# Cross-attention and mixture of experts: attended columns centred while they are copied, means added back later

## What is computed

```
energy    = (ctx Wq^T + bq) (ctx Wk^T + bk)^T                      # per batch, 256 x 256
x         = x + layernorm(x) @ softmax(energy)^T
logits    = layernorm(x) @ gate^T;  e = argmax;  slot = rank of the token in e (dropped from 160 on)
out[tok]  = x[tok] + prob * gelu(layernorm(x)[tok] @ wi[e]) @ wo[e]
```

## Time and profile before

| | before |
|---|---|
| runs | 110.72, 111.43, 111.35 us |
| the profiled execution, its own time | 110.13 us |
| its span on the core | 108.3 us |
| TensorE busy, share of the span | 101.4 us, 94% |
| VectorE, ScalarE, GpSimd busy | 33.2, 33.0, 31.0 us |
| granted TensorE clock, mean | 0.988 |

### The profile page before, as it was taken

How to read it: one execution, slowest core, us unless ns; L and a number is a source line. 1 busy time by engine, 2 the same in 40 slices (tenths; PEclk the granted TensorE clock), 3 DMA queues, 4 the chain that set the end, 5 groups by cost and what they waited for, 6 DMA issues and landing times.

```text
span 108.3 us, 1960 instructions
## 1 busy us (share of the span) xinstructions
PE 101.4 (94%) x744; PEld 89.9 (83%) x744; DVE 33.2 (31%) x135; ACT 33.0 (30%) x87; POOL 31.0 (29%) x58
## 2 busy tenths in 40 slices
PE   5999999989999989999999999999999999999910
PEld 5875987869999779998998998669989999988900
DVE  0055898999710143600510400220020010011210
ACT  4139678865651302341041041002302303200000
POOL 5710599677770000030200200303003003012550
PEclk9999999999999999999999999999999999999995
DMA  2989999999992879999999999960001001001100
GB/s 74 273 298 355 355 321 408 424 412 420 415 387 100 176 235 377 332 316 396 436 421 415 421 430 414 424 244 33 0 0 42 0 6 48 0 0 47 54 3 3
DMA packets 7713, 25.76 MB, mean 238 GB/s; under 512 B 912, under 2 KB 4245, under 8 KB 5656
## 3 DMA queue, kind: packets, MB, share of 16 engines
q1 hardware_dynamic: 6680, 23.39, 58.2%
q0 software_dynamic: 880, 2.12, 5.3%
q10 hardware_dynamic: 144, 0.13, 0.5%
HBM read 21.14 MB, written 4.76 MB: 239 GB/s over the span
## 4 chain that ended last, share of the span: by engine, by line
PE 75%; DMA 12%; POOL 3%; issue 2%; DVE 2%; SPq 2%; ACT 0%; ACTq 0%
PE ps L822 68%; DMA shared<-in_head 5%; PE ps L866 4%; DMA slots_dram<-rows,slot 4%; DMA rest<-slots_dram 3%; POOL slots_dram L339 2%; PE ps L819 2%; POOL out L377 1%; DVE rows L561 1%; SPq L218 1%; SPq L214 1%; DVE stats L619 0%; DVE stok L746 0%; ACT attended L388 0%; DVE y_end L798 0%
## 5 line engine op out<-in xcount | busy, mean ns | idle before, releaser
L822 PE MATMUL ps<-wo_sb,shared 128*32 128x128 f32 (+2 forms) x320 | 36.4, 337 | 0.0
L822 PE MATMUL ps<-shared,wi_sb 128*128 128x160 f32 x244 | 34.6, 299 | 0.0
L822 PEld LDWEIGHTS ps<-shared,wi_sb 128*128 128x128 f32 x244 | 33.6, 190 | 0.1
L822 PEld LDWEIGHTS ps<-wo_sb,shared 128*32 128x32 f32 (+1 forms) x320 | 29.2, 142 | 5.0 <-issue 0.7
L493 ACT ACTIVATE shared<-ps 128x480 f32<-128x480 f32 (+1 forms) x24 | 12.5, 526 | 48.9 <-PE ps L822 48.4
L370 POOL DMA_INDIRECT out<-y,got x9 | 8.8, 974 | 60.8 <-DVE y L780 44.1
L780 DVE SCALAR_TENSOR_TENSOR y<-ps,share,got 128x256 f32<-128x256 f32 x9 | 4.4, 484 | 48.1 <-PE ps L822 24.7
L822 PE MATMUL ps<-shared 128*128 128x256 f32 (+1 forms) x28 | 9.5, 481 | 0.1
L339 POOL DMA_INDIRECT slots_dram<-rows,slot x8 | 8.2, 1021 | 3.4 <-DVE slot L604 1.9
L822 PE MATMUL ps<-attended,shared 128*128 128x272 f32 x32 | 8.3, 398 | 0.5 <-ACT attended L388 0.5
L822 PEld LDWEIGHTS ps<-shared 128*128 128x128 f32 x28 | 6.0, 229 | 2.2 <-issue 1.0
(11 more groups left out here) (87 smaller groups left out, 72.3 us busy)
## 6 DMA issues: line engine op xcount, KB each, us to landing
wi_sb<-in_wi SPq DMA_DIRECT2D x8, 1024.0 KB, 15.6
wo_sb<-in_wo SPq DMA_DIRECT2D x8, 1024.0 KB, 18.9
slots_dram<-fill SPq DMA_DIRECT2D x1, 1300.0 KB, 12.6
shared<-in_xT SPq DMA_DIRECT2D x2, 512.0 KB, 7.3
out<-rows SPq DMA_DIRECT2D x4, 256.0 KB, 5.6
got<-slots_dram SPq DMA_DIRECT2D x1, 780.0 KB, 6.3
got<-slots_dram SPq DMA_DIRECT2D x4, 130.0 KB, 2.5
shared<-in_x SPq DMA_DIRECT2D x2, 256.0 KB, 4.0
```

The costliest lines, as they stand in the source:

```text
L822: return nc.tensor.matmul(dst, lhsT, rhs, start=(k == 0), stop=last)
```

## The change

The rows that leave `x1` have no mean any more. `idg` and `attended` get one more column beside the eight gate columns (`G` = 9), so that `at` also yields minus the mean of each attended row over its columns. VectorE copies that one column out of PSUM (`column_mean_of(b, c)`), and ScalarE adds it as a bias while it copies (`at`, now an Identity with a bias). GpSimd prepares mean minus input from `mv` alone, and `x1` subtracts it. `bn2`, `st2` and `token` are gone: ScalarE's `squared(n)` makes the sum of squares in one pass, `disp` takes the rows themselves, and the first expert's tokens are copied with no change of sign. The row's mean comes out of the extra column (`mean(b)`) and travels with the row. It is added back in two places: by VectorE to the rows read back from the slots (`full_row`), and by GpSimd to the eight row tiles, after the scatters have landed, before SyncE writes them to the output. `BY_LOG` is 1: batches 1 to 3 get their deviation through logarithm and exponential, only batch 0 through GpSimd. All four `turner` are built by VectorE. The lists of ScalarE, GpSimd, VectorE and TensorE are in another order.

```diff
...
-WIDE = H + 2 * E
-HALF = WIDE // 2
+
+G = E + 1
+HALF = P + G
+WIDE = 2 * HALF
...
-BY_LOG = 3
+BY_LOG = 1
...
             sp.dma_start(got[:, 0, :], by_rank[0:P, 0, :]).then_inc(got_zero, 16)
             sp.dma_start(got[:, 2:E, :], by_rank[0:P, 2:E, :]).then_inc(got_main, 16)
             sp.dma_start(rest[:, 1, :], by_rank[P:CAP, PER_STACK:E, :]).then_inc(rest_here[1], 16)
-            for b in range(B):
-                sp.dma_start(out_v[b], rows[:, 2 * b:2 * b + 2, 0:H]).then_inc(x1_out, 16)
             last_slots(0)
             last_slots(1)
+            for b in range(B):
+                sp.wait_ge(full_rows, 2 * b + 2)
+                sp.dma_start(out_v[b], rows[:, 2 * b:2 * b + 2, 0:H]).then_inc(x1_out, 16)
             for e in range(3, E):
...
+            nc.gpsimd.memset(fill[:, 0:H], 0.0).then_inc(fill_done, 1)
+            nc.gpsimd.memset(fill[:, H:ROW], 1.0).then_inc(fill_done, 1)
+            pool.wait_ge(fill_done, 2)
...
-            nc.gpsimd.memset(idg[:, HALF + E:], 0.0).then_inc(zeroed, 1)
+            nc.gpsimd.memset(idg[:, P + E:P + G], -1.0 / H).then_inc(ident_done, 1)
+            nc.gpsimd.memset(idg[:, P + G + E:HALF + G], -1.0 / H).then_inc(ident_done, 1)
+            nc.gpsimd.memset(attended[:, :, :, E:G], -2.0 / H).then_inc(means_put, 1)
+
+            nc.gpsimd.memset(rows[:, :, MEAN], H ** 0.5 * EPS ** 0.5).then_inc(eps_put, 1)
...
             def shifted_input(n):
-                pool.wait_ge(shift1_done, n // 4 + 1)
-                nc.gpsimd.tensor_scalar(x_sb[:, n, :], x_sb[:, n, :], 1.0, shift1[:, n:n + 1], ALU.mult,
+
+                pool.wait_ge(st1_done, n // 4 + 1)
+                nc.gpsimd.tensor_scalar(x_sb[:, n, :], x_sb[:, n, :], -1.0, mv[:, n, 0:1], ALU.mult,
                                         ALU.add).then_inc(xs_done, 1)
...
             def second_rstd(b):
-                pool.wait_ge(st2_done, b + 1)
-                if b == 0:
-                    pool.wait_ge(filled, 16)
+                pool.wait_ge(square_sums, 2 * b + 2)
                 pair = slice(2 * b, 2 * b + 2)
                 nc.gpsimd.tensor_tensor(rows[:, pair, RSTD], rows[:, pair, RSTD], minus_half[:, 0:2],
                                         ALU.pow).then_inc(rstd2_done, 1)
...
             def scatter(n):
 
+                if n == 0:
+                    pool.wait_ge(filled, 16)
                 if n % 2 == 0:
                     pool.wait_ge(numbered, n // 2 + 1)
+                    pool.wait_ge(mean_put, n // 2 + 1)
                     pool.wait_ge(row_ready[n // 2], 2)
...
-            put_gate()
-            first_rstd(0)
             shifted_input(0)
             shifted_input(1)
+            first_rstd(0)
+            put_gate()
             shifted_input(2)
-            first_rstd(1)
             shifted_input(3)
             shifted_input(4)
             shifted_input(5)
+            shifted_input(6)
             second_rstd(0)
-            shifted_input(6)
             shifted_input(7)
+            first_rstd(1)
             scatter(0)
-            second_rstd(1)
...
+
+
+            pool.wait_ge(scattered, 16 * NT)
+            pool.wait_ge(disp_done, 2)
+            for n in range(NT):
+                nc.gpsimd.tensor_scalar(rows[:, n, 0:H], rows[:, n, 0:H], 1.0, rows[:, n, MEAN:MEAN + 1], ALU.mult,
+                                        ALU.add).then_inc(full_rows, 1)
...
                     act.wait_ge(xm_done, 2 * (b - 1))
                 act.wait_ge(at_done, HC * b + c + 1)
-                copy(attended[:, b % 2, c, E:WIDE], p_at[c][:, E:WIDE]).then_inc(at_sb, 1)
-
-            def turn_by(b):
-
-                act.wait_ge(erec_done, b + 1)
-                act.wait_ge(at_done, HC * (b - 1))
-                for m in range(2):
-                    n = 2 * b + m
-                    nc.scalar.activation(turner[:, b % 2, m * HALF:(m + 1) * HALF], idg[:, m * HALF:(m + 1) * HALF],
-                                         ACT.Copy, scale=erec[:, n:n + 1]).then_inc(act_turner_done, 1)
+
+                act.wait_ge(column_means, HC * b + c + 1)
+                nc.scalar.activation(attended[:, b % 2, c, G:WIDE], p_at[c][:, G:WIDE], ACT.Identity,
+                                     bias=column_mean[:, b, c:c + 1]).then_inc(at_sb, 1)
...
                 pair = slice(2 * b, 2 * b + 2)
-                act.wait_ge(st2_done, b + 1)
+                act.wait_ge(square_sums, 2 * b + 2)
                 nc.scalar.activation(near[:, pair], rows[:, pair, RSTD], ACT.Ln).then_inc(log_done, 1)
                 act.wait_ge(log_done, b + 1 - BY_LOG)
...
-            def token(n):
-
-                act.wait_ge(st2_done, n // 2 + 1)
+            def squared(n):
+
+                act.wait_ge(x1_done, n + 1)
                 if n == 0:
-                    act.wait_ge(en_done, B)
-                nc.scalar.activation(tok[:, n, :], rows[:, n, 0:H], ACT.Identity, bias=rows[:, n, MEAN:MEAN + 1],
-                                     scale=-1.0).then_inc(tok_done, 1)
+                    act.wait_ge(eps_put, 1)
+                if n >= 2:
+                    act.wait_ge(square_sums, n - 1)
+                nc.scalar.activation(squares[:, n % 2, :], rows[:, n, 0:H + 1], ACT.Square, scale=H ** -0.5,
+                                     accum_out=rows[:, n, RSTD:RSTD + 1]).then_inc(square_sums, 1)
...
-            nc.scalar.activation(dispT[:, 1, 0, :], p_disp[1], ACT.Copy, scale=-1.0).then_inc(disp_sb[1], 1)
+            copy(dispT[:, 1, 0, :], p_disp[1]).then_inc(disp_sb[1], 1)
...
                 dve.wait_ge(erec_done, b + 1)
                 if b == 0:
                     dve.wait_ge(gate_done, 1)
-                    dve.wait_ge(ident_done, 2)
+                    dve.wait_ge(ident_done, 4)
+                if b >= 2:
+                    dve.wait_ge(at_done, HC * (b - 1))
                 nc.vector.tensor_tensor(per_half(turner[:, b % 2, :]), per_half(idg[:]),
                                         erec[:, pair_of(b)][:, :, None].to_broadcast([P, 2, HALF]),
                                         ALU.mult).then_inc(turner_done, 1)
 
+            def column_mean_of(b, c):
+
+                dve.wait_ge(at_done, HC * b + c + 1)
+                nc.vector.tensor_copy(column_mean[:, b, c:c + 1], p_at[c][:, HALF + E:HALF + G]).then_inc(column_means, 1)
+
             def x1(n):
+
+                dve.wait_ge(rstd1_done, n // 4 + 1)
                 dve.wait_ge(xm_done, n + 1)
                 dve.wait_ge(xs_done, n + 1)
-                nc.vector.scalar_tensor_tensor(halves(rows[:, n, 0:H]), halves(p_xm[n // 2 % 2][:, n % 2, 0:WIDE])[:, :, E:HALF],
+                nc.vector.scalar_tensor_tensor(halves(rows[:, n, 0:H]), halves(p_xm[n // 2 % 2][:, n % 2, 0:WIDE])[:, :, G:HALF],
                                                rstd1[:, n:n + 1], halves(x_sb[:, n, :]), ALU.mult,
-                                               ALU.add).then_inc(x1_done, 1)
+                                               ALU.subtract).then_inc(x1_done, 1)
...
-                nc.vector.tensor_tensor(logits[:, b, :, :], p_xm[b % 2][:, :, HALF:HALF + E], wide(rstd1[:, pair_of(b)]),
-                                        ALU.mult).then_inc(scaled_done, 1)
+                nc.vector.tensor_tensor(logits[:, b, :, :], p_xm[b % 2][:, :, HALF:HALF + G],
+                                        rstd1[:, pair_of(b)][:, :, None].to_broadcast([P, 2, G]), ALU.mult).then_inc(scaled_done, 1)
...
-            def bn2(n):
-                dve.wait_ge(x1_done, n + 1)
-                nc.vector.bn_stats(stats[:, 1, n, 0:6], rows[:, n, 0:H]).then_inc(bn2_done, 1)
-
-            def st2(b):
-                dve.wait_ge(bn2_done, 2 * b + 2)
-                for n in range(2 * b, 2 * b + 2):
-                    last = nc.vector.bn_aggr(rows[:, n, MEAN:RSTD + 1], stats[:, 1, n, :])
-                last.then_inc(st2_done, 1)
+            def mean(b):
+
+                dve.wait_ge(square_sums, 2 * b + 2)
+                dve.wait_ge(logits_done, b + 1)
+                dve.wait_ge(shift1_done, b // 2 + 1)
+                nc.vector.scalar_tensor_tensor(rows[:, pair_of(b), MEAN], logits[:, b, :, E], -0.5, shift1[:, pair_of(b)],
+                                               ALU.mult, ALU.add).then_inc(mean_put, 1)
...
+            gate()
+            mx(0)
...
+            column_mean_of(0, 0)
...
-                nc.vector.tensor_scalar(stok[:, i % 2, :], row[:, 0:H], row[:, MEAN:MEAN + 1], row[:, RSTD:RSTD + 1],
-                                        ALU.subtract, ALU.mult).then_inc(stok_done, 1)
+                nc.vector.tensor_scalar(stok[:, i % 2, :], row[:, 0:H], row[:, RSTD:RSTD + 1], None,
+                                        ALU.mult).then_inc(stok_done, 1)
...
+            def full_row(n):
+
+                t = OUT_TILES[n]
+                if n == 0:
+                    dve.wait_ge(got_zero, 16)
+                elif n == 1:
+                    dve.wait_ge(got_one, 16)
```

(27 more changed lines are left out.)

168 lines of the change are left out of this document (89 added, 79 removed).

## The result

The changed kernel takes 113.29 us (median of four executions, 112.69 to 114.8) against 111.23 us (median of four, 110.72 to 111.43): a ratio of 1.017, 95% interval 1.0125 to 1.0215. It is slower, by 2.1 us. I had forecast 110.35 us in a range of 109.4 to 111.6.

A forecast was written before the change was run, and what follows sets the result against it. The last scatter's landing was taken as the bound, its chain 0.9 us later than TensorE's. Landing 1.0 us earlier, all else 0, gave 111.35 - 1.0 = 110.35 us, range 109.4 to 111.6.

The forecast's parts named there:

- The walk up to the routing's end: Routing on TensorE and VectorE: `x1(7)` at 24.95, `row_numbers(3)` at 28.0, last `disp` ended at 28.95, 1.2 us earlier.
- The one after `row_numbers` starts 0.43 us after its start ... scatter 4 at 26.0: GpSimd's scatters: scatter 4 at 26.0, then 1.25 or 1.3 us apart, the last at 29.8, 1.25 us earlier than 31.08.
- The sentence on `first_rstd(1)` ending as `row_numbers(0)` starts: GpSimd ahead of the first scatter: `first_rstd(1)` stands there now and ends at 20.1, when `row_numbers(0)` starts.
- I take ... a landing at 34.1: Last scatter's landing: 0.25 us of the 1.25 us gain lost beside streaming weights, so 1.0 us earlier.
- My first rival: At the scatters' landing: the weights hold it, gain 0 to 0.5 us, time 110.85 to 111.35; chance 0.2.
- from 33 to 35 q0 alone was left: DMA queues before the landing: only the scatters' queue still moved then, 0.09 MB at 13.1%.
- The rule that I cited against the change: DMA engines go round their queues packet by packet; in the extreme the landing gains 0 instead of 1.0 us.
- Nothing else is on the path: Beyond landing and TensorE: adding means, output and expert 3's weights are hidden, so 110.13 - 1.0 = 109.1 us.
- The third rival: VectorE's routing: small operations cost 0.2 us, not 0.1, `row_numbers(3)` at 29.8, time 111.75 to 112.5; chance 0.13.

The follow-up runs named there:

- `a_again2`: The changed kernel with nothing altered, measured again on a later occasion: 110.19 us against 110.1 us of before, ratio 1.000.
- `b_again`: The kernel before with nothing altered, run again for its trace on a later occasion: 111.74 us in one execution.

## Why the prediction was wrong

Undisturbed, the forecast of 1.0 us gained turned into 0 at two steps, the issue of the scatters and their landing.

**The walk up to the routing's end** was close: measured from the start of `at(0)` (10.88 before, 10.14 after, 10.76 in `a_again2`), `x1(7)` comes at 14.6 where I had 14.07, `row_numbers(2)` at 15.2 where I had 14.67, `chosen(3)` at 16.5 where I had 16.0. Half a microsecond of 16 too early, in both traces alike. TensorE started `mm1(0)` 0.64 us earlier and not 1.2.

**"The one after `row_numbers` starts 0.43 us after its start ... scatter 4 at 26.0"** failed. I used that distance for scatter 4 and never walked scatters 0 to 3. They stand on the same engine at 1.28 us each, the third waited for ScalarE's `expz(1)`, which ended 1.1 us later than before, and from there GpSimd had no pause left: 27.08, and 30.92 for the last, 0.16 us gained and not 1.25. ScalarE's list was never walked for what a scatter needs. The sentence on `first_rstd(1)` ending as `row_numbers(0)` starts asked only whether GpSimd is free, not what else the scatters wait for.

**"I take ... a landing at 34.1"** failed: 35.8 and 35.1. My first rival was right, the weights hold the landing, and I gave it 0.2. The premise "from 33 to 35 q0 alone was left" was a misreading. The view of the earlier trace rows for 33 to 35 us has one line more:

```profile
q1 hardware_dynamic: 5, 0.02, 2.0%
```

The weights' last packet ended at 33.9 us in that trace, not before 33, and the scatters landed 1.2 us behind it. The share of 2.0% is small, but a landing waits for the last packet and not for the mean. Issuing the scatter earlier does not move the weights: their last packet ended at 33.0 to 34.7 us in the changed kernel and its variants where no signal was late, at 33.2 and 33.9 in the kernel before. The rule that I cited against the change, of the Trainium skill, "DMA: Bandwidth & Descriptors", Queues, rings and completion order, fits: in the trace of before two of the weights' packets, at 33.28 and 33.60, stand among the scatters' packets of 33.25 to 34.57.

**"Nothing else is on the path"** held from `dT(1)` on: the 71.2 us from there to the end are those of the kernel before, so adding the means, the output and the weights of expert 3 are hidden, as priced. It missed ScalarE's wait for the same landing between two gelus. That wait costs 0.4 to 1.25 us in the traces without late signals where TensorE is early enough, but only time that TensorE would have spent waiting at the transposes.

**What I had not thought of** made the first measurement slower rather than equal: the late signal of `rk(3)`, 2.5 us, and the half clock behind it, 1.1 us. The third rival was for slower and had another mechanism (small operations at 0.2 us); where none waits they start 0.08 us apart (seven of them from 24.14 to 24.73 in the first trace of the changed kernel). And part of the comparison was in the frame itself: the profiled execution of before, at 110.13, had no late signal, while `b_again`, from an occasion with a median of 111.16, had two of 0.5 us at the end. I had noted that the median lay 1.2 us above the profiled execution and asked no further.

## To carry to other kernels

Walk every instruction of the engine that issues the transfers, from its first one; a distance taken from one that had slack is no price once they stand back to back. For each transfer ask what all it waits for, not only the input that comes last today. Before an earlier issue is booked as an earlier landing, find whose packets are the last ones ahead of the landing: where they are another queue's, the landing stays. And before a gap is explained by a program's waits, compare the end of the work with the record of the signal: where both kernels show it on one day and neither on another, it is not the change.

## What the runs showed of the hardware

- A signal of TensorE can be late by 0.5 to 2.5 us with nothing else waiting. On the three later occasions where it happened (1, 3 and 5) it happened in every kernel traced, at the same three signals, and the traces of such occasions hold 1298 to 1377 records of semaphores' changes instead of 1457 to 1493. Every timed execution here is a recorded one, so that the recording itself holds the signals is possible; nothing here can show or exclude it.
- After about 2.4 us without a matmul the granted clock was at half speed for the next 2.5 us in some executions and at full speed in others of the same kernel.
- A scatter on GpSimd that waits for its last input itself started 0.30 us after it; behind a separate wait instruction for the same input, 0.87 us (0.79 in the case of `expz(1)`).
- The last scatter landed 0.9 to 1.7 us behind the last packet of the weights' queue in 16 of 17 traces, whether it was issued at 30.3 or at 32.3 us, and took 2.5 us from its issue to the first load where no weights moved.
